# A fused convolution and scan kernel: wider last-stage pieces, part of the last stage taken into the scan loop, and a first stage in blocks of 128 positions

## The reference

```
# layer 0, per image: a linear attention without softmax
theta, phi, g = conv1x1(x, w_theta), conv1x1(x, w_phi), conv1x1(x, w_g)      # 128 channels each
out = (theta^T phi / 3136) g          # so only phi g^T, a 128 x 128 matrix, is needed: one 256 x 256 map per image
x = batchnorm(conv1x1(out, w_rec)) + x

# layer 1: two Mamba blocks on the same numbers, read as 4*56 sequences of 56 tokens with 256 features
xz = u @ in_w.T;  x, z = split(xz)                     # 512 each
x = silu(causal conv of 4 taps along the sequence)
dt, B, C = x @ xp_w.T                                   # 16 + 16 + 16
dt = softplus(dt @ dt_w.T + dt_b)
h = exp(dt * A) * h + dt * x * B                        # a scan over 56 tokens, 512 channels x 16 states
y = (h . C + x * D) * silu(z) @ out_w.T
out = conv1x1(concat(y1, y2), cat_w) + cat_b + x        # the last convolution, 512 to 256 channels
```

## Time and profile before

| engine | busy us | share of the span |
|---|---|---|
| PE (matmul) | 4836.0 | 86% |
| PEld (weight load) | 3541.9 | 63% |
| DVE | 5064.4 | 90% |
| ACT | 3547.9 | 63% |
| POOL | 5064.0 | 90% |

### The profile page before, as it was taken

The page is one execution under the profiler, slowest core; times in us unless marked ns, Lnnn a source line. Parts: engine busy times, 40 slices in busy tenths (PEclk is TensorE's granted clock), DMA queues, the critical chain, the costliest instruction groups (busy, mean ns, idle before and its releaser), DMA issues. The chain is left out here.

```text
span 5615.2 us, 71207 instructions
## 1 busy us (share of the span) xinstructions
PE 4836.0 (86%) x26046; PEld 3541.9 (63%) x26046; DVE 5064.4 (90%) x3469; ACT 3547.9 (63%) x5534; POOL 5064.0 (90%) x2582
## 2 busy tenths in 40 slices
PE   8888888888888888888788888889989898888887
PEld 7746566656666565656556656666666666666664
DVE  4469999999999999999999999999999999999992
ACT  0067676766666676767566767666666666766662
POOL 0079999999999999999999999999999999999992
PEclk9989999999999999999899999999999999999999
DMA  4232323232232323232323232333232424242423
GB/s 153 102 109 67 116 67 112 77 102 91 89 108 71 116 67 116 67 112 78 111 67 116 67 112 81 109 104 114 93 125 87 134 80 138 77 144 75 140 70 127
DMA packets 242753, 560.65 MB, mean 100 GB/s; under 512 B 29314, under 2 KB 116226, under 8 KB 241252
## 3 DMA queue, kind: packets, MB, share of 16 engines
q1 hardware_dynamic: 230804, 528.00, 29.2%
q10 hardware_dynamic: 11600, 28.10, 1.3%
HBM read 497.86 MB, written 58.15 MB: 99 GB/s over the span
## 5 line engine op out<-in xcount | busy, mean ns | idle before, releaser
L1058 POOL TENSOR_TENSOR dbx<-dtx,b_all 128x896 f32<-128x896 f32 x1792 | 3701.3, 2102 | 0.1
L986 DVE TENSOR_TENSOR_SCAN mamba_ps<-mamba_ps,dbx 128x896 f32<-128x896 f32 x1232 | 2481.8, 2014 | 106.4 <-ACT mamba_ps L860 63.5
L805 PE MATMUL mamba_ps<-ident,hc 128*112 128x128 f32 x14336 | 1867.5, 282 | 167.0 <-POOL hc L1065 135.9
L805 PEld LDWEIGHTS mamba_ps<-ident,hc 128*112 128x112 f32 x14336 | 1668.7, 138 | 507.4 <-issue 255.3
L860 ACT ACTIVATE mamba_ps<-dt,w 128x448 f32<-128x448 f32 x1792 | 1067.7, 629 | 727.3 <-DVE hc L993 580.8
L993 DVE TENSOR_TENSOR hc<-mamba_ps,c_all 128x896 f32<-128x896 f32 x1232 | 1341.7, 1089 | 137.8 <-DVE mamba_ps L986 3.9
L860 ACT ACTIVATE mamba_ps<-dt,a_next 128x448 f32<-128x448 f32 x1792 | 1067.4, 629 | 626.4 <-DVE hc L993 500.9
L1065 POOL TENSOR_TENSOR hc<-hc,c_all 128x896 f32<-128x896 f32 x560 | 1176.0, 2100 | 130.8 <-DVE hc L986 130.4
L986 DVE TENSOR_TENSOR_SCAN hc<-mamba_ps,dbx 128x896 f32<-128x896 f32 x560 | 1129.1, 2016 | 51.0 <-ACT mamba_ps L860 50.9
L702 PE MATMUL mamba_ps<-u,w 128*128 128x448 f32 x1792 | 799.6, 584 | 203.8 <-ACT sz L883 109.3
L713 PE MATMUL mamba_ps<-x,taps 128*128 128x448 f32 (+3 forms) x1792 | 727.0, 550 | 117.2 <-ACT x L874 108.3
(11 more groups left out here) (107 smaller groups left out, 3105.9 us busy)
## 6 DMA issues: line engine op xcount, KB each, us to landing
b_all<-bc_scratch SPq DMA_DIRECT2D x448, 448.0 KB, 5.5
c_all<-bc_scratch SPq DMA_DIRECT2D x448, 448.0 KB, 4.8
u<-u_scratch SPq DMA_DIRECT2D x56, 448.0 KB, 3.3
y_scratch<-ytok SPq DMA_DIRECT2D x56, 448.0 KB, 3.3
src<-y_scratch SPq DMA_DIRECT2D x80, 224.0 KB, 4.5
u_scratch<-ub ACTq DMA_DIRECT2D x28, 448.0 KB, 4.6
xb<-in_x ACTq DMA_DIRECT2D x3, 3136.0 KB, 10.7
src<-in_x SPq DMA_DIRECT2D x40, 224.0 KB, 5.2
```

The costliest lines, as they stand in the source:

```text
L805: ins = nc.tensor.matmul(y_ps[j % 2][:, c * 128:(c + 1) * 128], hc[g][:, e * T + c * TCH:e * T + (c + 1) * TCH], ident[:, :], start=False, ...
L986: nc.vector.tensor_tensor_scan(dst, h, dbx[n % BX_RING][:, :], 0.0, ALU.mult, ALU.add).then_inc(scan_done, 1)
L1058: nc.gpsimd.tensor_tensor(view(dbx[n % BX_RING], 0, [[T, 2], [1, T]]), view(dtx, j * T, [[0, 2], [1, T]]), view(b_all, 2 * g * T, [[T, 2], ...
```

## The change

First stage: HALF is 128, so an image has 12 pairs and one block of 64 (TAIL); buffers and banks of pairs alternate on through the images; the batch-norm chain is a generator of which one step runs behind each pair of image 0 from pair 1 on; the first weight transpositions ride one pair earlier; each image's result is stored by two transfers, the lower 128 channels from ACT's queue and the upper from SP's.

Loop: the pieces of the last convolution are 448 columns wide (f0, f1), the loads of a piece come once per tile, ahead of `store`, and its store at the end of SP's tile. It starts in tile 29: tiles 29 to 35 compute the part of image 3 that needs only block 1 (blocks 0, 1, 4, 5: y1 and x) and store it to `part_dram`. The table has new slots, `hc` is a ring of 6 by slot number, POOL weighs slot 27 instead of 30 and 5 slots late instead of 3, three gates and two y copies move, and the new taps and skip matrices are made by ACT, a group of four behind each of the decays 0 to 3 and 31, with a semaphore count per group.

Last stage: one whole tile (image 2's last) and for image 3 the two blocks of y2, to which DVE adds the stored part. SP loads y2 and stores; ACT loads the parts.

```diff
-HALF = NPOS // 28
+HALF = 128
 SCHEDULE = {
-    "z0": (0, 0), "x0": (0, 0), "x1": (0, 2), "z1": (0, 3), "z2": (2, 4), "z3": (2, 5), "c0": (4, 5), "c1": (6, 8),
-    "y3": (7, None), "x2": (9, 10), "x3": (10, 11), "c2": (11, 12), "c3": (12, 13), "y0": (13, None), "out0": (15, 17), "xp": (16, 19),
-    "out1": (18, 20), "dt0": (19, 22), "dt1": (19, 22), "fa0": (21, 23), "dt2": (21, 23), "dt3": (22, 24), "fa1": (23, 26), "y1": (24, None),
-    "y2": (31, None), "fb0": (31, 31), "fb1": (31, 31),
+    "x0": (0, 0), "x1": (0, 0), "z0": (0, 1), "z1": (0, 2), "z2": (1, 4), "c0": (4, 6), "z3": (4, 6), "c1": (6, 8),
+    "y3": (9, None), "x2": (9, 10), "x3": (12, 12), "c2": (12, 12), "c3": (12, 14), "y0": (13, None), "out0": (16, 18), "xp": (17, 18),
+    "out1": (17, 20), "dt0": (19, 21), "dt1": (21, 23), "dt2": (21, 23), "dt3": (23, 23), "y1": (25, None), "f0": (26, 26), "f1": (26, 29),
+    "y2": (31, None),
 }
-TAKE_Y_AT = {5: 3, 13: 0, 22: 1, 28: 2}
-GATE_AT = {8: 3, 15: 0, 25: 1, 29: 2}
+TAKE_Y_AT = {5: 3, 14: 0, 22: 1, 29: 2}
+GATE_AT = {8: 3, 14: 0, 24: 1, 30: 2}
-FIN, FIN_FROM = T // 2, TILES + TPB + 1
-FIN_TILES = range(FIN_FROM, 2 * TILES)
+PART_FROM, FIN_FROM = TILES + 1, TILES + TPB + 1
+FIN_TILES = range(PART_FROM, 2 * TILES)
-BX_RING, HC_RING = 5, 8
+BX_RING, HC_RING = 5, 6
-    return n % (2 * GP) in (1, 4, 6, 10, 14)
+    return n % SLOTS in (1, 4, 6, 10, 14, 17, 20, 22, 26, 27)
-POOL_LAG, SUMS_LAG = 3, 4
+POOL_LAG, SUMS_LAG = 5, 4
...
-    PAIRS, UT = 14, 13
+    PAIRS, UT = 13, 13
+    TAIL = NPOS % (2 * HALF)
...
+        def store_u(queue, b, k):
+            queue.dma_start(u_dram[b * TPB:(b + 1) * TPB].rearrange("t p (k n) -> k p t n", k=2)[k],
+                            ub[b % 2][:, k * NPOS:(k + 1) * NPOS].rearrange("p (t n) -> p t n", t=TPB)).then_inc(u_stored[b % 2], 16)
...
                         take_pair(b, i)
+                        if b == 0 and i >= 1:
+                            next(steps, None)
...
+                    for m in range(1 if part else 2):
+                        sp.dma_start(s[:, 2 * m:2 * m + 2, :], y_img[m][b][:, :, i * T:(i + 1) * T]).then_inc(src_ready, 16)
+                    sp.dma_start(s[:, 4:6, :], x_in[b]...[:, :, i * T:(i + 1) * T]).then_inc(src_ready, 16)
...
-                        if g == 2:
-                            between(t - 1)
...
+                    blocks = (0, 1, 4, 5) if part else range(6)
...
+                def make_taps(j):                                  # now on ACT
+                    ...
+                    for k in range(j * DCONV, (j + 1) * DCONV):
+                        ins = nc.scalar.activation(taps[:, k * 128:(k + 1) * 128], ident[:, :], ACT.Copy, scale=w[:, W_CW + k:W_CW + k + 1])
+                    ins.then_inc(taps_ready, 1)
...
                         decays(SLOTS * t + n)
+                        if t == CHANGE - 1 and n < DB:
+                            make_taps(n)
+                        if t == CHANGE - 1 and n == SLOTS - 1:
+                            make_skip()
...
 def finish(...):                                                  # new body, shortened
+            sync:    cat_t <- cat_dram; y1[i] <- piece i of y2, i in 0..6; then out <- part[i] when taken
+            scalar:  part[i] <- part_dram[i], i in 0..6, and behind i == 3 the four loads of the whole tile
+            tensor:  for i in 0..6: 2 x 2 matmuls of y1[i]; behind i == 4: 2 x 6 matmuls of the whole tile
+            vector:  part[i] = bank + part[i], two additions per i
```

More of the change, by code:

```diff
@@ L243, in _ @@
                 sp.dma_start(cat_dram, cat_t[:, :]).then_inc(w_stored, 16)
+                for b in range(2):
+                    sp.wait_ge(ut_taken, UT * (b + 1))
+                    store_u(sp, b, 1)
                 sp.wait_ge(copied, M1[-1] + 1)
@@ L311, in add_pair @@
                         upto(pe, k_dve, 4 * (b - 1) + 1)
[L312 to L316, removed]
+                    rows = HALF if i < PAIRS - 1 else TAIL
+                    for h in range(2 if i < PAIRS - 1 else 1):
+                        s = pg[(b + i) % 2]
+                        last = nc.tensor.matmul(bank(2)[:, 0:CMID], s[0:rows, h * 256 + 128:h * 256 + 256],
+                                                s[0:rows, h * 256:h * 256 + 128],
+                                                start=(i == 0 and h == 0), stop=(i == PAIRS - 1))
                     last.then_inc(mt_step, 1)
@@ L442, in first_half @@
                             take_turn(n)
-                        if i == 13 and b in (0, 2):
+                        if i == PAIRS - 1 and b in (0, 2):
                             take_a(b // 2)
+                    for _ in steps:
+                        pass
                     dve.wait_ge(mt_step, PAIRS * (b + 1))
@@ L1086, in _, with finish @@
                                 weigh(SLOTS * t + n)
-def finish(nc, x_in, y_dram, k_dram, cat_dram, out):
-    b0, n0 = fin_of(2 * TILES)
-    jobs = [(b0, i) for i in range(n0 // T, TPB)] + [(b, i) for b in range(b0 + 1, BATCH) for i in range(TPB)]
-    batches = list(range(b0, BATCH))
+def finish(nc, x_in, y_dram, k_dram, cat_dram, part_dram, out):
+    last, left = BATCH - 1, fin_of(2 * TILES)
     with ExitStack() as ctx:
@@ new lines, in _ @@
+                for i in range(TPB):
+                    sp.wait_ge(taken, i + 1)
+                    sp.dma_start(piece(image(out[last]), i), halves(part[i])).then_inc(stored, 16)
+                sp.wait_ge(stored, 16 * TPB)
+            @block.scalar
+            def _(act):
+                for i in range(TPB):
+                    act.dma_start(halves(part[i]), part_dram[i]).then_inc(part_ready[i], 16)
+                    if i == 3:
+                        b, n, _ = left
+                        s = whole[:, :].rearrange("p (k n) -> p k n", k=6)
+                        act.dma_start(now[:, :], k_dram[b]).then_inc(whole_ready, 16)
+                        for m in range(2):
+                            act.dma_start(s[:, 2 * m:2 * m + 2, :], piece(y_img[m][b], n)).then_inc(whole_ready, 16)
+                        act.dma_start(s[:, 4:6, :], piece(image(x_in[b]), n)).then_inc(whole_ready, 16)
+                act.wait_ge(whole_made, 1)
+                for oc in range(2):
+                    ins = nc.scalar.activation(done[:, oc * T:(oc + 1) * T], whole_bank(oc), ACT.Identity, bias=now[:, 2 * CH + oc:2 * CH + oc + 1])
+                ins.then_inc(whole_taken, 1)
+                act.wait_ge(whole_taken, 1)
+                act.dma_start(piece(image(out[b]), n), halves(done)).then_inc(whole_taken, 16)
+                act.wait_ge(whole_taken, 17)
@@ L1139, in _ @@
+            @block.vector
+            def _(dve):
+                for i in range(TPB):
+                    dve.wait_ge(part_ready[i], 16)
+                    dve.wait_ge(made, i + 1)
                     for oc in range(2):
-                        o = ((j % 4) * 2 + oc) * 512
-                        ins = nc.scalar.activation(res[j][:, oc * T:(oc + 1) * T], ps[:, o:o + T], ACT.Identity,
-                                                   bias=now[:, 2 * CH + oc:2 * CH + oc + 1])
+                        h = part[i][:, oc * T:(oc + 1) * T]
+                        ins = nc.vector.tensor_tensor(h, out_bank(i, oc), h, ALU.add)
```

256 lines of the change are left out of this document (125 added, 131 removed).

## The result

After the change the kernel takes 5513.41 us (median of 4 runs, 5511.31 to 5514.35) against 5613.37 us on the same chip; the ratio is 0.9821, interval 0.9804 to 0.9838. Forecast were 5455 us and a range of 5425 to 5536. The profiled execution spans 5509.5 us where the one before spans 5615.2.

What follows compares the result with a forecast made beforehand. DVE and POOL were both taken as full in the scan loop. Terms -20.7 - 21.0 - 80.6 + 6.0 - 43 = -159.3 led from median 5613.23 to 5454, stated as 5455 us; own range 5425 to 5490, with rivals to 5536.

Steps and rivals of the forecast that it cites:

- What bounds the kernel: Scan loop: DVE and POOL both full; DVE's prices per slot give 89.9 us a tile, POOL busy 90.25.
- First stage: Before the loop: interleaved chain 7.7 us, 1.5 fewer pairs in 4 batches 13.0; term -20.7, bounds -12 and -24.
- Two stores: First stage's end: store by two transfers counted at 0; 4.3 us if a second queue doubled the rate.
- Weight-change tile: Tile of 111.96 us: taps and skip matrices leave DVE for ACT; term -21.0, bounds -12 and -21.6.
- The stall of the last 19: Last 19 periods: earlier requests and pieces at slot 26 cut 95.24 us to 91.0; term -80.6, bounds -94 and -52.
- rival A: Last-convolution pieces: PE late at slot 26, 3 us in 27 tiles, 5536 us; chance 0.12.
- D: Last 19 tiles: the stall only moves, behind slot 26 or 29, tiles stay at 95.2, 5536 us; chance 0.06.
- The other 35 periods: Loop's other tiles: 90.83 to 91.0 us each, POOL's lead correcting itself; term +6.0, bounds -18 and +58.
- rival B: SP's order: B's load for slot 4 queued behind C's wait for POOL's weighing 27; 1 us, 55 periods, 5510; chance 0.08.
- Rival C: Slot 17: PE's sums late for the ring of 6; 5620 us with PE held up 3.3 us; chance 0.05.
- Last stage: End of kernel: 80 matmul instructions in place of 192, two DVE additions; term -43, bounds -36 and -46.

Runs made afterwards that it cites:

- act_taps: Kernel before, with only the new taps and skip matrices at the weight change made by ACT instead of DVE: 5596.43 us, ratio 0.9964.
- early_loads: Kernel before, with SP requesting the second last-convolution piece's data behind slot pair 0 instead of pair 2: 5545.28 us, ratio 0.9875.
- b_ahead: Changed kernel, with SP requesting the B row of the next slot pair before the C row of the current one: 5463.86 us, ratio 0.9727.
- lag4: Changed kernel, with POOL weighing 4 slots late instead of 5: 5456.13 us, ratio 0.9709.
- x_ahead: Changed kernel, with PE running x0 and x1 ahead of the sum of slot 27: 5518.76 us, ratio 0.9823.
- both: Changed kernel with the edits of b_ahead and x_ahead together: 5459.43 us, ratio 0.9713.
- lag4_raws_first: lag4, with raw weights requested ahead of batch-norm vectors and the chain run two steps per pair from pair 4: 5450.4 us, ratio 0.9706.

## Why the forecast came out as it did, step by step

- **What bounds the kernel**: right. DVE's and POOL's prices per slot hold to 0.03 us after the change, and the floor that they give was reached once nothing else stood in the way (90.76 to 90.87 in five experiments; forecast 91.0).
- **First stage**, -20.7: the interleaved chain and the 1.5 pairs less were right in kind. In the profiled execution -24.5; in six others 258.0 to 259.8, which is -13.9 to -15.6. The case priced as the low bound (-12, "PE waits for the loads instead") is the usual one: the wait for raw weights, put at 1.4 us, is 6.9 to 8.4 us, and behind it PE is slow again. Nothing in the median of the change shows this cleanly, since the loop scatters by as much.
- **Two stores**: counted at 0, worth 0.3. By the Trainium skill's rule (DMA: Bandwidth & Descriptors, "Issuing engines are not separate DMA queues") it is 0 but for issue time, and the trace agrees: 0.3, not 4.3.
- **Weight-change tile**, -21.0: -19.4, of which the tile's own share is right (act_taps: 111.96 to 91.70, -20.3) and 0.9 is the period's loss. A group of four matrices took ACT 1.26 us, inside the bounds of 0 and 1.8:

```profile
2863.69 1.26 ACT L917 ACTIVATE skip<-ident,w 128x128 f32<-128x128 f32 x4
```

  That is 0.315 each; the estimate from the Trainium skill's page VectorE: DVE Perf Modes ("The TRN2 errata") was 0.29, 0.02 less.
- **The stall of the last 19**, -80.6: the mechanism was right (early_loads shows it alone), and so was the schedule: the pieces at slot 26 find their data, ACT takes them without a wait, and neither rival A (PE late) nor D (the stall moves) appears. A tile's piece in the loop after the change:

```profile
4504.82 1.29 PE L793 MATMUL mamba_ps<-src,now 128*128 128x448 f32 x3
4505.94 3.17 PE L793 MATMUL mamba_ps<-src,cat_tt 128*128 128x448 f32 x8
4507.46 0.61 ACT L948 ACTIVATE res<-mamba_ps,now 128x448 f32<-128x448 f32 x1
```

  The term is -61.9 because the new period is 91.98, not 91.0: 18.6 us that belong to the next point.
- **The other 35 periods**, +6.0: +36.5. This is the step that failed. The prediction said "But then DVE is the slower, the lead grows, and the wait goes: it corrects itself". That argument holds only if POOL can pull ahead. It can't: near the start of each tile POOL waits for B rows that SP may only ask for after POOL's own late weighing, a loop of POOL, SP and a DMA whose length doesn't depend on DVE. The loop was seen, as rival B, and even priced (1 us in 55 periods, 5510, where 5513 came out), but given 0.08. It was looked for at slot 4, and there it nearly fits: three operations of 2.05 are 6.15 us of cover, against 0.4 us from the request of the C row to that of the B row and 5.5 us of landing, 5.9 in all. What the rival left out is the row behind. Slot 5 has one operation more of cover, but its row is requested 1.0 us later and lands in 7.9 us, so 1.1 us a tile are missing. The 5.5 of the earlier trace rows is one number for all 448 rows and hides those that leave in a burst. b_ahead and lag4 show that the held requests are the cause. x_ahead shows that the late x0 doesn't set the period while they stand; without them it costs 0.07 to 0.17 us a period (b_ahead against both).
- **Rival C**, the ring of 6 at slot 17: not there. Slots 16 to 20 last what their prices say on the mean of the tiles (3.25 with a wait for an activation, 1.94, 3.15, 3.16, 1.93).
- **Tile 55**: +6.7, not in the sum at all. Moving the pieces from slot 31 to 26 took PE's work away just where it kept the clock up for the tail.
- **Last stage**, -43: -42.9. PE's part is 33.2 us instead of 74.17:

```profile
5472.07 18.16 PE fin_ps L1173 x40
5490.23 9.02 PE fin_ps L1182 x24
5499.25 6.03 PE fin_ps L1173 x16
```

  -41.0 (forecast -42.1), for the first matmuls run after 14 us of idling; the first load's way is 1.9 us shorter (forecast 1).

The range held the result only because it had been drawn out to the prices of rivals A and D, 5536, which didn't come; without rivals it ended at 5490, and rival B's own price was 5510. With POOL's lag at 4 the kernel takes 5456.13 us, 1 us from the 5455 forecast, but part of that is luck. In its profile the first stage misses its term by 5 us and tile 55 by another 5, and the periods, some 10 us shorter in all than forecast, and 2 us less of set-up make up for it.

## What to carry to other kernels

When an engine's work is moved later in its order, look for every transfer whose request waits for that work, and for what is queued behind that request: a buffer's release through an in-order DMA queue is part of the loop. One held request holds all behind it, which then leave together and land one after the other. So look at each of them against its own cover, with the landing time that it has in the burst (7.9 us here) and not the median of all (5.3). "The lead grows until the wait goes" is an argument only when no wait in the circle belongs to the engine that is to lead. And before a large change is credited, try its parts alone: moving one request earlier gave 70 us, and one constant of the change itself cost 57.

## What the runs showed of the hardware that was not expected

- A row spread to 128 partitions (448 KB) lands 5.6 us after its request when it is the first behind the held one; the next three B rows of the same burst, with C rows between them, take 7.9, 8.9 and 9.7 us (means in the changed kernel).
- A load of 32 KB landed in 7.4 us in one execution and in 14.3 to 15.1 us in ten others, with its request at nearly the same place (19.93, and 20.17 to 21.08 us) and 3.2 MB asked for by another engine's queue some 2 us later.
- PE's clock in the gaps of the last tile. After the change the group of 8 behind a single wait of 2.36 us already runs at half rate (1.96 us instead of 1.09), though PE had been busy before it. In lag4_raws_first the same group behind a wait of the same length takes 1.09, and the next one, behind 2.08 us more, 1.96. The 32 matmuls that follow take 10.10 and 9.08 us instead of 7.16. Some 0.9 to 1.7 us of unneeded matmuls in each gap kept the clock up.
- Where the loop hangs on a landing time, profiled executions of the same loop differ by 9 us in its 55 periods (5047.1, 5053.2 and 5055.9); in the five kernels in which x0 isn't late either they agree to 1.4 us (4994.5 to 4995.9). b_ahead, with the wait removed but x0 late, takes 5004.2.
